# A 3x3/5x5 and quadratic convolution pair: the order in which the first stage's taps are summed, turned and copied

## What is computed

```
x = x + L0(gn(x), w3, b3, w5, b5, wr, br)
x = x + L1(gn(x), filters)

L0: y3 = conv3x3(x, w3) + b3;  y5 = conv5x5(x, w5) + b5
    out = wr[:, 0] * y5 + sum over 9 shifts s of wr[:, 1 + s] * shift_s(y3) + br
L1: spot = (1, the 9 pixels of a 3x3 patch);  out = sum over (i, j) of filters[o, c, i, j] * spot_i * spot_j
```

## Time and profile before

| what | us |
|---|---|
| timed, three runs | 327.13, 328.39, 328.31 |
| median | 328.31 |
| span of the profiled execution | 325.1 |
| TensorE busy in the span | 294.5 (91%) |
| VectorE busy | 206.6 (64%) |
| ScalarE busy | 103.0 (32%) |
| GpSimd busy | 39.0 (12%) |

### The profile page before, as it was taken

One profiled execution on the slowest core, in us unless ns is written; L12 is line 12 of the kernel. 1 busy time (PEld: TensorE's weight loads), 2 busy tenths in 40 slices (PEclk: granted clock), 3 DMA queues, 4 the chain that ended last, 5 costly groups with the idle time before them and its releaser, 6 DMA issues.

```text
span 325.1 us, 14576 instructions
## 1 busy us (share of the span) xinstructions
PE 294.5 (91%) x6976; PEld 144.3 (44%) x6976; DVE 206.6 (64%) x176; ACT 103.0 (32%) x166; POOL 39.0 (12%) x100
## 2 busy tenths in 40 slices
PE   0678989699997999997999999999999999999990
PEld 0224434344444364454455546545643654544650
DVE  1879999987980006999999844293005496982121
ACT  5412006888069992014000042890000000000181
POOL 6999820000000001000000000000000000000000
PEclk9999999999997999999899999999999999999997
DMA  6944000000000000000000000451000000000047
GB/s 202 381 106 103 4 2 3 2 5 4 2 2 4 2 4 2 4 2 2 4 2 4 2 4 4 108 123 36 4 2 2 4 4 2 4 2 4 4 99 162
DMA packets 7627, 11.52 MB, mean 35 GB/s; under 512 B 5392, under 2 KB 5520, under 8 KB 7440
## 3 DMA queue, kind: packets, MB, share of 16 engines
q1 hardware_dynamic: 5104, 9.59, 10.9%
q10 hardware_dynamic: 2464, 1.01, 1.3%
HBM read 6.40 MB, written 4.19 MB: 33 GB/s over the span
## 4 chain that ended last, share of the span: by engine, by line
PE 51%; issue 11%; DVE 7%; DVEq 0%; POOL 0%; ACT 0%
PE acc L808 51%; DVE product L735 4%; DVE stats L648 1%; DVE plane L663 0%; DVE product L693 0%; DVEq L94 0%; DVE raw L716 0%; DVE mean_var L653 0%; POOL product L317 0%; DVE raw L718 0%; DVE offset L723 0%; POOL product L318 0%; DVE norm L657 0%; DVE norm L661 0%; ACT norm L419 0%
## 5 line engine op out<-in xcount | busy, mean ns | idle before, releaser
L808 PE MATMUL acc<-product,weight 32*32 32x512 f32 (+1 forms) x4416 | 183.7, 604 | 2.1 <-DVE product L735 2.1
L735 DVE TENSOR_TENSOR product<-plane 128x4096 f32<-128x4096 f32 x24 | 105.0, 4423 | 66.6 <-PE acc L808 38.0
L808 PEld LDWEIGHTS acc<-product,weight 32*32 32x32 f32 (+1 forms) x4416 | 95.0, 112 | 87.4 <-issue 62.7
L475 ACT ACTIVATE raw<-acc,offset_by_strip 32x512 f32<-32x512 f32 x36 | 24.4, 678 | 99.6 <-PE acc L808 99.1
L445 ACT ACTIVATE raw<-product 32x512 f32<-32x512 f32 x60 | 40.8, 680 | 3.1 <-DVE product L600 2.3
L835 PE MATMUL acc<-product,middle 32*64 32x512 f32 (+1 forms) x576 | 28.6, 596 | 2.5 <-DVE middle L588 1.4
L808 PE MATMUL acc<-plane,weight 32*32 32x512 f32 (+1 forms) x512 | 27.4, 628 | 0.6 <-DVE product L600 0.6
L686 DVE TENSOR_SCALAR raw<-acc,offset_by_strip 32x512 f32<-32x512 f32 x12 | 9.1, 757 | 24.1 <-PE acc L808 23.8
L570 DVE TENSOR_TENSOR product<-plane 128x2048 f32<-128x2048 f32 (+1 forms) x8 | 22.4, 2811 | 0.0
L648 DVE BATCH_NORM_STATS2 stats<-raw 128x6 f32<-128x512 f32 x32 | 19.7, 679 | 2.6 <-DMA raw<-in_x 2.4
L502 ACT ACTIVATE product<-plane 128x4096 f32<-128x4096 f32 x2 | 7.3, 3636 | 39.8 <-PE acc L808 37.0
(11 more groups left out here) (91 smaller groups left out, 152.2 us busy)
## 6 DMA issues: line engine op xcount, KB each, us to landing
raw<-in_x SPq DMA_DIRECT2D x8, 512.0 KB, 8.4
out<-raw SPq DMA_DIRECT2D x12, 256.0 KB, 3.0
filters_in<-in_L_conv_filters SPq DMA_DIRECT2D x4, 400.0 KB, 4.0
out<-product SPq DMA_DIRECT2D x8, 64.0 KB, 2.4
out<-product ACTq DMA_DIRECT2D x8, 64.0 KB, 2.7
w_in<-in_L_conv_w ACTq DMA_DIRECT2D x4, 100.0 KB, 3.7
w_in<-in_L_conv_w ACTq DMA_DIRECT2D x2, 36.0 KB, 1.9
w_in<-in_L_conv_w SPq DMA_DIRECT2D x2, 36.0 KB, 2.2
```

The costliest lines, as they stand in the source:

```text
L475: last = nc.scalar.activation(strip_rows(g, r, s, h), strip_acc(s, h, r), ACT.Identity, bias=offset_by_strip[32 * s:32 * s + 32, r, g:g + 1])
L735: nc.vector.tensor_tensor(product_rows(n), inner(g, 0, H), shifted(g, PRODUCTS[k]), ALU.mult)\
L808: return nc.tensor.matmul(acc[32 * s:32 * (s + strips), h, r, :], weights[32 * r:32 * r + 32, t:t + strips, :] .rearrange("p t c -> p (t c ...
```

## The change

1. ScalarE writes the scaled 5x5 taps into a new tile, `w5_taps`, already in folded order, in two operations (columns 3 and 4, then 0 to 2). GpSimd adds them in two contiguous adds in place of five strided ones.
2. GpSimd's 14 border memsets move from behind the nine shift adds to ahead of them. The add of columns 3 and 4 and the pair move to behind the sixth shift add (columns 3 and 4 are complete by then); columns 0 to 2 follow the ninth.
3. VectorE turns the pair inside `normalise(0)`, between the variance and the wait for its square root, no longer behind the plane.
4. VectorE runs `outer_taps` ahead of `halve total`, no longer behind it.
5. The copies of column 2 for both groups, so far VectorE's (L581), are made by ScalarE in `copy_taps`; the counts of `taps_copied` that others wait for rise accordingly.

```diff
+        w5_taps = sb("w5_taps", [128, TAPS0, C])
...
             nc.gpsimd.memset(folded[:, :, :], 0.0).then_inc(shift_folded, 1)
+            for g in range(NG):
+                for name in ("total", "step", "left", "right"):
+                    if (g, name) != (1, "left"):
+                        pad_half(g, name).then_inc(padded, 1)
             pool.wait_ge(shift_folded, 1)
+
+            def add_five(a, b):
+                part = folded[:, 5 * a:5 * b, :]
+                nc.gpsimd.tensor_tensor(part, part, w5_taps[:, 5 * a:5 * b, :], ALU.add).then_inc(columns_added, 1)
+
...
                 nc.gpsimd.tensor_tensor(part, part, three, ALU.add).then_inc(shift_folded, 1)
                 pool.wait_ge(shift_folded, n + 2)
-            for g in range(NG):
-                for name in ("total", "step", "left", "right"):
-                    if (g, name) != (1, "left"):
-                        pad_half(g, name).then_inc(padded, 1)
-            pool.wait_ge(taps5_ready, 1)
-            for n, x in enumerate((3, 4, 0, 1, 2)):
-                part = folded[:, 5 * x:5 * x + 5, :]
-                nc.gpsimd.tensor_tensor(part, part, w5_in[:, :].rearrange("p (c y x) -> p x y c", y=5, x=5)[:, x, :, :],
-                                        ALU.add).then_inc(columns_added, 1)
-                if n == 1:
-                    pool.wait_ge(columns_added, 2)
+                if n == 5:
+
+                    pool.wait_ge(taps5_ready, 1)
+                    add_five(3, 5)
+                    pool.wait_ge(columns_added, 1)
                     nc.gpsimd.tensor_tensor(folded[:, PAIR_AT:PAIR_AT + 5, :], folded[:, 15:20, :], folded[:, 20:25, :],
                                             ALU.add).then_inc(pair_added, 1)
+            pool.wait_ge(taps5_ready, 2)
+            add_five(0, 3)
...
             def copy_taps():
                 act.wait_ge(outer_turned, 1)
+                nc.scalar.activation(middle0[0][:, 0, :, :], weight0[:, 10:15, :], ACT.Copy).then_inc(taps_copied, 1)
                 nc.scalar.activation(half_one[:, :, :], weight0[:, 5:10, :], ACT.Copy, scale=0.5).then_inc(taps_copied, 1)
                 nc.scalar.activation(minus_one[:, :, :], weight0[:, 15:20, :], ACT.Copy, scale=-1.0)\
                   .then_inc(taps_copied, 1)
+                nc.scalar.activation(middle0[1][:, 0, :, :], weight0[:, 10:15, :], ACT.Copy).then_inc(taps_copied, 1)
...
-            nc.scalar.activation(w5_in[:, :], w5_in[:, :], ACT.Copy, scale=wr_in[:, 0:1]).then_inc(taps5_ready, 1)
+            for a, b in ((3, 5), (0, 3)):
+                nc.scalar.activation(w5_taps[:, 5 * a:5 * b, :].rearrange("p (x y) c -> p x y c", y=5),
+                                     w5_in[:, :].rearrange("p (c y x) -> p x y c", y=5, x=5)[:, a:b, :, :],
+                                     ACT.Copy, scale=wr_in[:, 0:1]).then_inc(taps5_ready, 1)
...
             def outer_taps():
-                dve.wait_ge(columns_added, 5)
+                dve.wait_ge(columns_added, 2)
...
             def middle_taps(g):
 
-                step(nc.vector.tensor_copy(middle0[g][:, 0, :, :], weight0[:, 10:15, :]))
+                dve.wait_ge(taps_copied, (1, 4)[g])
...
-                dve.wait_ge(taps_copied, 1)
+                dve.wait_ge(taps_copied, 2)
...
                 nc.vector.tensor_scalar(norm[:, 0:1], mean_var[:, 1:2], GN_EPS, None, ALU.add).then_inc(var_ready, 1)
+                if phase == 0:
+                    dve.wait_ge(pair_added, 1)
+                    turn(PAIR_AT, PAIR_AT + 5).then_inc(pair_ready, 1)
                 dve.wait_ge(std_ready, phase + 1)
...
-                if phase == 0:
-                    dve.wait_ge(pair_added, 1)
-                    turn(PAIR_AT, PAIR_AT + 5).then_inc(pair_ready, 1)
...
             dve.wait_ge(padded, 4 * NG - 1)
+            outer_taps()
             halve(0, "total")
-            outer_taps()
             middle_taps(0)
...
-                pe.wait_ge(taps_copied, 2)
+                pe.wait_ge(taps_copied, 3)
```

## The result

| executions | kernel before | changed kernel |
|---|---|---|
| median of 16 | 328.35 us | 326.19 us |
| mean (one changed execution of 1568.67 left out) | 328.00 us | 325.49 us |
| lowest, highest (the same one left out) | 325.71, 329.61 | 321.56, 328.58 |
| ratio, with its 95% interval | | 0.987 (0.9835 to 0.9906) |

The ratio overstates the gain, since its comparison leaves out executions more than 1.5% above a kernel's fastest, here 6 of the changed kernel's 15 and none of the other's. By the medians above it is 0.993. Two later sessions have medians of 327.73 against 328.30 us and 326.15 against 326.89, both 0.998. Over all sessions the mean of 46 changed executions is 326.2 us, of 107 of the kernel before 327.7. So the change made the kernel faster by 1.5 us on average, 0.45%, with a 95% interval of 0.8 to 2.1 us.

What follows compares the result with a forecast made beforehand. TensorE was taken to bound the kernel, with its gap at 45.29 us pinned to a DMA. The front counted 0 and the copy 0.27, so 328.31 - 0.27 = 328.0 us, range 327.2 to 328.9.

Steps and rivals of the forecast that it cites:

- the wait ahead of "right": TensorE's gap before 45.29 us: VectorE's halve "right" stands behind GpSimd's filter sums; gap grows from 1.11 to about 2.2.
- The front: Work up to TensorE's "total": starts 1.1 us earlier (0.3 to 2.4), but worth 0 in the end.
- ScalarE: mis-sized: ScalarE's scaling in folded order, reading every 25th element: 0.46 us for the first 320, hidden.
- The pin: Halve "right" ends at 45.19 us however early VectorE reaches it, fixed by the filters' DMA through GpSimd's sums.
- The copy's 0.27: Second group's middle taps on VectorE's run to the edges: without their copy, 0.27 us saved that stays.
- Rival A: At halve "right", VectorE gets the port after one GpSimd add; edges start near 58.1, time 325.0 us; chance 0.21.
- The estimate of 1 us lost to the sums still queued: Within Rival A: VectorE's run to `finish_odd` starts 4.1 us earlier, loses about 1 in three waits of 0.35.
- Rival B: At the front, GpSimd's adds and edge subtracts starve VectorE; "total" later than 28.0, time 329.3 us; chance 0.05.
- Rival C: TensorE's clock falls behind the longer gap at 45 us: 1.7 lost, 0.1 comes through, 328.4 us; chance 0.07.

Runs made afterwards that it cites:

- e17: The changed kernel, unaltered, traced again: 323.87 us.
- e5: The changed kernel with VectorE made to wait for all filter sums before halve "right": median 328.39 us, ratio 1.0009.
- e6: The kernel before, with VectorE made to wait for all filter sums before halve "right": median 327.34 us, ratio 1.0018.
- e3: The kernel before, with GpSimd's filter sums held until halve "total" of the second group is done: median 324.48 us, ratio 0.9907.
- e7: The kernel before, with a wait of GpSimd on itself behind every filter sum: 324.63 us, ratio 0.9919.
- e2: The changed kernel with GpSimd's filter sums held until halve "total" of the second group is done: median 322.77 us, ratio 0.9875.
- e4: The changed kernel with a wait of GpSimd on itself behind every filter sum: 324.02 us, ratio 0.9891.
- e9: The changed kernel with one single wait of GpSimd on itself, behind the 15th of 27 filter sums: 324.07 us, ratio 0.9882.
- e16: The changed kernel with one single wait of GpSimd on itself, behind the 20th of 27 filter sums: median 325.19 us, ratio 0.991.
- e1: The changed kernel, unaltered, traced again: 326.53 us.
- e8: The changed kernel, unaltered, traced again: 326.43 us.
- e11: The changed kernel, unaltered, traced again: 326.23 us.
- e12: The changed kernel, unaltered, traced again: 327.89 us.
- e14: The changed kernel, unaltered, traced again: 326.22 us.
- e18: The changed kernel, unaltered, traced again: 326.89 us.
- e13: The changed kernel, unaltered, traced again: 328.57 us.
- e15: The changed kernel, unaltered, traced again: 328.54 us.

## Why the prediction was wrong

The forecast was 328.0 us, within 327.2 to 328.9, and the median came out at 326.19. **The step that failed is the wait ahead of "right"**: "The gap at 45.29 is therefore pinned to a DMA: halve "right" ends at 45.19 whether VectorE reaches it at 37 or at 42." That held in nine of ten traces ("right" ended at 44.13 to 45.62) and failed in e17, where "right" ended at 40.58 with 15 of the 27 sums not yet done; by the times it fails in about a third of the executions. The rest of the reckoning stood, as follows.

**The front: right.** The pair add ended at 12.72 (12.9 forecast), its turn started at 14.41 (near 14), the plane was ready at 18.29 (18.2), "next" started at 18.64 (18.35); what set that was probably ScalarE's part of the plane, done at 18.55 (16.87 + 1.68), later than VectorE's. "Total" started 1.57 us earlier, against 1.1 with bounds of 0.3 and 2.4; the gap of the middle taps had closed altogether. VectorE's small norm operation at 15.47 did take 1.05 us behind the 480-element add, as bounded.

The Trainium skill, "SBUF — State Buffer", section "Who interferes with whom", has two-input VectorE operations collide with GpSimd's reads; this row is such a collision with operands of one element a partition, and the trace agrees.

**ScalarE: mis-sized, without effect.** The 320 elements took 0.91 us, not 0.46, and the 480 took 1.22, where 800 contiguous ones took 0.96. The first was done at 11.12, 0.15 before GpSimd's add started: the cover was used up but for that, as much by the later start (10.21 in place of 9.68, behind the landing of the 5x5 taps) as by the price.

**The pin: right where it holds.** In the execution profiled first "right" ended at 45.44 (45.2 forecast), with a gap of 2.82 (over 2). In e5 and e6, where it always holds, front or no front makes no gain. The 33 of 46 executions that are not under 324.7 average 327.3 (a few in which VectorE got in may be among them), and those of before 327.7: 0.4 less, with an uncertainty of 0.4, where 0.27 was forecast. The copy's 0.27 can be seen by itself: from the end of "right" to the end of `finish_odd(0)` 16.11 us before and 15.85 after.

**Rival A: where the failed step was defended.** It had the right mechanism, the right place and nearly the right price: 325.0 us and edges at 58.1 were forecast, 57.20 was traced, and the quick executions lie at 321.56 to 324.66. What was wrong was to treat the pin as a fact about the kernel. "VectorE got in between none of them", from one trace, and "three timed runs within 1.3 us show no execution where it did" were put against A as if they decided for every execution and for the changed kernel. They said only that it is rare in the kernel before, and that much is right: the forms of it in which "right" is not shut out (e3, e7) were under 325.0 us in 16 of 24 executions, the unaltered kernel in 2 of 107. At a granted clock of 0.980 to 0.982 all nine executions of e3 and e7 took 325.02 us or less, and all 25 of the unaltered kernel 325.55 or more. With the change, the forms that are open by their rows or times (e2, e4, e9) were under 324.7 in 15 of 18 executions, the unaltered one in 13 of 46: an estimate from the two shares is that about a third get in. The 13 lie 3.9 us below the other 33 (323.4 and 327.3), which takes 1.1 off the mean, and with the 0.4 of the others that is the 1.5 by which the mean over all sessions fell; the first session, with 7 of its 15 under 324.7, fell by 2.5. So the median of 326.19 hangs on how many quick executions a session happens to have: it was 327.73 in the second. The estimate of 1 us lost to the sums still queued was too high too: "far" took 2.52 in place of 2.28.

The range was too narrow beside that. It was set by three executions 1.26 us apart, and the 107 of the kernel before run from 324.77 to 331.43. Also, a timed execution lasts 1.7 to 1.8 us longer than its own span, not 3.2: the median and the profiled span were of different executions. The difference that was forecast did not depend on it.

**What decides the draw stays open.** Of 15 traced cases in which VectorE came upon a run of adds with no wait just ahead, it got in at the first boundary in three (e3, e9, e17) and was passed by 7 to 15 adds in twelve (7 in e16, up to the wait). By the starts in the traces it asked 0.00, 0.04 and 0.16 us into the running add in the three, and 0.03 to 0.36 in the others, so that moment doesn't separate them. One thing is regular: where VectorE asked for its next such operation while a sum was held behind the last one, it came in behind that sum each time, with no wait of GpSimd between the two (e1, e3, e8, e9, e11, e12, e16 and e17; e17's "far" is one). Why it happens oftener with the change, which asks at 38.1 in place of 39.56 among the same adds, isn't settled either, and no run takes the five parts of the change one by one; that it does happen oftener is in the times.

The Trainium skill, "SBUF — State Buffer", section "SBUF: two separate sides", says that of a two-input VectorE operation and a GpSimd operation whichever starts first has the pair for its whole instruction while the other fully blocks. At GpSimd's waits (e4, e7, e16) the runs agree: VectorE blocks until the add that runs is over, then GpSimd's next one blocks. In an unbroken run of adds they mostly disagree with it, read as first come, first served: in the execution profiled first VectorE had asked before each of fifteen adds began (from 38.09 to 43.29, 0.35 each) and was passed by all of them.

**Rival B** did not occur: "total" started at 23.75, not after 28.0. **Rival C** did, in the profiled execution: behind the gap of 2.82 the granted clock fell. From the view by windows (start and end, length, TensorE, weight load, VectorE, ScalarE, GpSimd, then granted clock, DMA):

```profile
45.50:50.50 5.00, 4.96 (x64) 1.97 (x72) 4.55 (x9) 1.24 (x2) 0.00 (x0) 0.69 0.01 3
61.40:69.00 7.60, 5.94 (x256) 3.35 (x248) 7.46 (x10) 5.87 (x15) 0.00 (x0) 0.78 0.02 5
```

It was 0.69 there, as in the earlier trace rows, and it cost what C said: the 64 products took 5.17 us, 1.48 more than the 3.69 of before, and the gap before the edges, 1.60 before, is gone: they started at 61.43, where before it was 61.44. The second row shows a further fall, behind a gap of 1.66 before 65.22, where the kernel before, with a gap of 1.33, kept 1.00 from 61.4 to 69; so the profiled span is longer than the one of before. Where the clock held (e1, e11, e12, e14, e18) that gap before the edges is 1.44 to 1.47, forecast as 1.3. With "right" shut out, the clock fell behind its gap in four of nine traces of the unaltered changed kernel, so 0.07 was too little for C. In e5 9 of 12 executions had a mean granted clock of 0.974 or less, in e6 one; that this is the longer gap's doing is likely but not shown.

## What to carry to other kernels

One trace is one draw: where two engines contend for something, and one of them loses by microseconds without a reason that the program gives, look at how the times of many executions are spread before calling it a property of the kernel. A long unbroken run of GpSimd's adds beside VectorE's two-input operations is worth breaking up with waits (327.4 to 324.6 us in the kernel before, its session's median against e7), or moving to where VectorE has none due. Work saved ahead of a pin is worth nothing while the pin holds (e5 against e6) and something once it gives (by the means 1.0 and 1.4 us here, e4 against e7 and e2 against e3), so price both.

## What the runs showed of the hardware

- GpSimd's adds without waits between them shut a two-input VectorE operation out for 3.35 us in the kernel before and for 5.07 (7.35 - 2.28) with the change, or let it in after one, from one execution of the same program to the next. Behind a wait of GpSimd for its own result VectorE was let in every time (e4, e7, e16), and so it was behind a sum that was itself held (eight of eight).
- ScalarE reading every 25th element took 2.5 to 2.8 ns an element (0.91 us for 320, 1.22 for 480), contiguous 1.2 (0.96 for 800).
- The length of TensorE's gap ahead of "right" did not tell whether the granted clock would fall behind it. It fell after 2.14, 2.65, 2.76, 2.78 and 2.82 us (e8, e13, e5, e15 and the execution profiled first: the 64 products took 5.17 to 5.39 us), and held after 1.73, 2.23, 2.43, 2.81 and 2.93 (e12, e11, e1, e14, e18: 3.69 us).
